# An attention and expert block on one core: P V products in groups of eight matmuls, eight P buffers, one set of exp sums, denominators at half 6

## The chip, the cores and the metric
The kernel runs on one core of one Trainium2 chip. The metric is the device time of one execution in microseconds (us). TensorE (PE) does the matmuls, VectorE (DVE) and ScalarE (ACT) read their results, GpSimd (POOL) adds, and SyncE (SP) issues most of the DMAs.

## The reference, cut to what matters
```python
# x: 4 x 1024 x 512 f32, 16 heads of 32; wq, wk, wv, wo: 512 x 512; 8 experts of rank 64
scores = einsum('bqhd,bkhd->bhqk', x @ wq.T, x @ wk.T)
att = einsum('bhqk,bkhd->bqhd', softmax(scores), x @ wv.T) @ wo.T
x = layernorm(x + att)
expert = argmax(softmax(x @ Wr.T + br)); weight = max(softmax(...))
y = ((x @ A[expert].T) @ B[expert].T) / 64 * weight
out = layernorm(x + y)
```

## The kernel before, in words
**Slots, units, halves.** The attention is done in 32 slots (4 batches of 8 head pairs). A slot has 16 units: for each of its 8 blocks of 128 keys, one unit for each head of the pair. A unit is 128 keys by 1024 queries and has two halves of 512 queries, so a slot has 32 halves and the kernel 1024. Every engine runs its own program, written out as a loop over the same halves, and semaphores tie them together.

**What a half holds on PE** (loop at lines 528 to 540): the scores matmul of this half (`score`, L493, records at L500) into one of two banks; one matmul for the row maxima of a later slot (`max_item`, L483, records at L490), 40 halves ahead, into one of three banks; in every fourth half (3, 7, 11, ...) an `out_block` (L503, records at L512): four matmuls that multiply one key block of P with V, each writing 32 of the 128 rows of the bank `pv` (two heads, two halves of the queries); and the pieces that a planner has put there (`AT`): projections Q, K, V (L400, L411), output projection (L422, L430), expert stages (L438 to L463), four chunks of one matmul each for most of them. The profile shows every f32 matmul of these as two passes, so an `out_block` has eight records and a chunk two; the matmuls for scores and maxima have one.

**The planner.** `PLAN` gives each slot three lists of pieces, one for each of `SEGMENTS` (L44), halves 0 to 10, 10 to 26 and 26 to 32; the pieces of a list are spread evenly over the halves of their segment, and `rooms` (L97) says how much each segment of a slot gets. Two pieces are pinned: `den` (L467) of the slot before at half 10, and `max_t` (L476) of the next slot at half 26. All pieces take turns on two banks `w`, and each waits until the piece two before it has been read out.

**Around the scores.** ACT reads the scores of a half and writes exp into P (`exp`, L560, records at L565), which has `NP` = 6 buffers of one unit. Before it overwrites one it waits for the P V products of that unit and for POOL's addition of it (`adds_until`, L226). POOL adds the P tiles of a slot into `Psum`, one running sum for each head (`add`, L348, 14 additions a slot, records at L354 and L358). `Psum` has two sets that slots use in turn. `den` multiplies the two sums with ones on PE (L472), ACT copies the result (`copy_den`, L585), DVE takes reciprocals in four pieces (L694) 2, 3, 5 and 6 halves later, and multiplies the copied `pv` with them (`normalise`, L698, two pieces) at `norm_half` (L223): 8 halves after `den`, or, for the first slot of a batch, at the start of the second slot behind it.

**The maxima.** DVE reduces each bank of L490 (L676). After the 32nd maximum of a slot (its matmul is issued at half 23 of the slot before) DVE combines them (L679) and writes the two parts of the negated maxima, `nm` (L684, L686). `max_t` transposes `nm` on PE at half 26 (L478), ACT copies it, and SP's DMA puts it into the stack that the scores of the next slot read.

Of the kernel before, what the change touches and what calls it, by code (L numbers as in the profile page):

```python
# [6 lines left out]
def build_attention_lora_moe_block(nc, xT, x, wqT, wkT, wvT, woT, aT, bT, wrT, br, out):  # L7
# [8 lines left out]
    D, TOK = xT.shape  # L16
    B, S, _ = x.shape
# [4 lines left out]
    KT = D // 128  # L22
    KB = S // 128
    PAIRS = H // 2
    QUADS = H // 4
# [6 lines left out]
    KS = 3 * HD + 2  # L32
    NP, NMX = 6, 3
    LEAD = 4
# [8 lines left out]
    WEIGHT = {"t1": 2, "t2": 2, "lg": 4, "den": 0, "max_t": 0}  # L43
    SEGMENTS = ((0, 10), (10, 26), (26, 32))  # L44

# [41 lines left out]
    for batch in range(B):  # L87
        at, final = PAIRS * batch, batch + 1 == B
        if batch == 0:
            PLAN[at] = (qks(0, 8, 1), qks(0, 9, 2), qks(0, 11, 1))  # L90
            PLAN[at + 1] = (qks(0, 12, 1), qks(0, 13, 2), qks(0, 15, 1))
        else:
            PLAN[at] = (tiles("v", batch, 4, 2), tiles("v", batch, 6, 2) + tiles("o", batch - 1, 0, 1), tiles("o", batch - 1, 1, 1))
            PLAN[at + 1] = (tiles("o", batch - 1, 2, 2), tiles("o", batch - 1, 4, 3), tiles("o", batch - 1, 7, 1))
        fill = qks(batch + 1, 0, 14) if not final else []
        pieces = expert_pieces(batch - 1, fill) if batch else fill
        rooms = ([2, 3, 1] if batch else [0, 4, 2]) + [2, 3, 1] * 4  # L97
        parts_of = spread(pieces, rooms)
        for n in range(5):
            PLAN[at + 2 + n] = tuple(parts_of[3 * n:3 * n + 3])  # L100
        PLAN[at + 7] = (tiles("part", 0, 0, 2), tiles("part", 0, 2, 4), tiles("part", 0, 6, 2)) if final else \
            (qks(batch + 1, 14, 2), tiles("v", batch + 1, 0, 3), tiles("v", batch + 1, 3, 1))

# [36 lines left out]
    with ctx:  # L140
# [16 lines left out]
        stack0, stack1 = sb("stack0", [128, 3, 2, S], f32r), sb("stack1", [128, 2, 2, S], f32r)  # L157
        V, P, Psum = sb("V", [128, KB, D]), sb("P", [128, NP, S]), sb("Psum", [128, 2, 2, S])
        attT = sb("attT", [128, KT, S])
# [174 lines left out]
        def _(pool):  # L334
# [13 lines left out]
            def add(s, k):  # L348
                unit, i = UNITS * s + k, k % 2
                pool.wait_ge(exp_done, 2 * unit + 2)  # L350
                if k < 4:
                    if s > 1:
                        pool.wait_ge(den_done, s - 1)
                    pool.tensor_tensor(Psum[:, s % 2, i, :], P[:, (unit - 2) % NP, :], P[:, unit % NP, :],  # L354
                                       ALU.add).then_inc(add_done, 1)
                else:
                    pool.wait_ge(add_done, ADDS * s + k - 3)
                    pool.tensor_tensor(Psum[:, s % 2, i, :], Psum[:, s % 2, i, :], P[:, unit % NP, :],  # L358
                                       ALU.add).then_inc(add_done, 1)
# [26 lines left out]
        def _(pe):  # L386
# [80 lines left out]
            def den(s, _, bank):  # L467
                pe.wait_ge(add_done, ADDS * (s + 1))
                for c in range(2):
                    for i in range(2):  # L470
                        at = HD * (2 * c + i)
                        done = pe.matmul(bank[at:at + HD, :], ones[:, :], Psum[:, s % 2, i, 512 * c:512 * c + 512],  # L472
                                         start=True, stop=True)
# [28 lines left out]

            def out_block(s, kb):  # L503
                pe.wait_ge(exp_done, 2 * (UNITS * s + 2 * kb + 2))
                if s % PAIRS == 0:
                    pe.wait_ge(v_done, KB * (s // PAIRS) + kb + 1)
                if kb == 0 and s:
                    pe.wait_ge(pv_copied, s)
                for c in range(2):
                    for i in range(2):  # L510
                        at, head = HD * (2 * c + i), 2 * (s % PAIRS) + i
                        done = pe.matmul(pv[at:at + HD, :], V[:, kb, HD * head:HD * head + HD],  # L512
                                         P[:, (UNITS * s + 2 * kb + i) % NP, 512 * c:512 * c + 512],
                                         start=(kb == 0), stop=(kb == KB - 1))
                done.then_inc(pv_done, 1)
# [12 lines left out]
            for half in range(HALVES * SLOTS):  # L528
# [5 lines left out]
                if c == 1 and k == 1 and s:  # L534
                    out_block(s - 1, KB - 1)
                if c == 1 and k % 2 == 1 and k >= 3:
                    out_block(s, (k - 3) // 2)
                for kind, n, chunk in AT.get(half, ()):
                    bank = begin((kind, n), False) if chunk == 0 else BANK[kind, n]
                    KIND[kind](n, chunk, bank)  # L540
            out_block(LAST, KB - 1)
            pe.wait_ge(exp_done, 2 * UNITS * SLOTS)
# [11 lines left out]
        def _(act):  # L554
# [5 lines left out]
            def exp(unit, c):  # L560
                if c == 0 and unit >= NP:
                    act.wait_ge(pv_done, (unit - NP) // 2 + 1)
                    act.wait_ge(add_done, adds_until(unit - NP))
# [9 lines left out]
            def copy_v(n):  # L573
                act.wait_ge(v_ready, n + 1)
                if n >= KB:
                    act.wait_ge(pv_done, KB * (PAIRS * (n // KB) - 1) + n % KB + 1)
                act.activation(V[:, n % KB, :], BANK["v", n][:, :], ACT.Copy).then_inc(v_done, 1)

            def copy_out(s):
                act.wait_ge(pv_done, KB * (s + 1))  # L580
                if s:
# [275 lines left out]
```

## Time and profile before
| | us |
|---|---|
| median of 3 runs (lowest, highest) | 1752.55 (1750.02, 1756.64) |
| the profiled execution | 1753.8 |
| its span, first to last instruction | 1751.9 |

A row of the timeline has the start in us, the duration in us, the engine, the line of the kernel, the operation with what it writes and reads, and how many records are merged into it; the bracket behind it is the idle time of that engine before it and who ended it. Rows of the kind PE are matmuls, whose ends are modelled, so distances between starts are used here rather than durations. Rows of a stretch give the busy time of each engine in it, then the granted clock of TensorE as a share of 2.4 GHz.

### The profile page before, as it was taken

The numbers are of one execution on the slowest core, as the hardware profiler recorded it, in microseconds if no ns is written. First come the engines' busy times: TensorE is split into PE (matmuls) and PEld (weight loads), VectorE is DVE, ScalarE is ACT, GpSimd is POOL, SyncE is SP. The second block draws the span as 40 slices with busy tenths as digits, with TensorE's granted clock in tenths as the row PEclk, the third lists the DMA queues.
The fourth block names the chain that finished last, engine by engine and source line by source line (L and its number), as shares of the span: only waits on it lengthen the run. The fifth ranks groups of instructions, "written<-read, shape, count | busy, mean of one in ns | idle before, by whom it ended". The sixth has DMA issues, their size and how long they took to land.

```text
span 1751.9 us, 19084 instructions
## 1 busy us (share of the span) xinstructions
PE 1610.9 (92%) x6432; PEld 765.0 (44%) x6432; DVE 1159.7 (66%) x1875; ACT 772.1 (44%) x1409; POOL 1109.0 (63%) x591
## 2 busy tenths in 40 slices
PE   5979899999999998899999999889999898889897
PEld 2434344444444444444444444444444444443353
DVE  1656777776676667866676776677666777776542
ACT  1134445454444444445445444444544544445322
POOL 1057777887676666566677765557767866768610
PEclk9989999999999999999999999999999999999999
DMA  7333432342032221135231122321313112210001
GB/s 239 97 121 91 134 95 72 86 114 60 20 84 61 73 73 57 40 92 148 51 85 41 34 84 61 85 50 65 116 37 85 38 37 49 49 31 14 0 1 48
DMA packets 64799, 123.40 MB, mean 70 GB/s; under 512 B 5296, under 2 KB 22720, under 8 KB 64704
## 3 DMA queue, kind: packets, MB, share of 16 engines
q1 hardware_dynamic: 61440, 116.94, 24.0%
q0 software_dynamic: 1152, 4.22, 0.7%
q10 hardware_dynamic: 2112, 1.05, 0.2%
q8 instruction: 51, 0.84, 0.2%
q14 instruction: 44, 0.36, 0.1%
HBM read 79.71 MB, written 41.94 MB: 69 GB/s over the span
## 4 chain that ended last, share of the span: by engine, by line
PE 72%; DVE 18%; issue 5%; POOL 2%; DMA 1%; ACT 1%; SPq 0%; ACTq 0%; POOLq 0%; DVEq 0%
PE w L400 12%; PE sc L500 12%; PE pv L512 12%; PE mx L490 11%; DVE mxc L676 6%; PE w L411 6%; PE w L422 5%; PE w L463 4%; PE w L450 4%; DVE attT L704 3%; DVE rden L696 2%; POOL Psum L358 2%; DVE split L691 1%; DMA wqk_s<-wkT 1%; PE w L444 1%
## 5 line engine op out<-in xcount | busy, mean ns | idle before, releaser
L358 POOL TENSOR_TENSOR Psum<-Psum,P 128x1024 f32<-128x1024 f32 x384 | 912.7, 2389 | 241.0 <-ACT P L565 239.6
L676 DVE TENSOR_REDUCE mxc<-mx 128x1 f32<-128x512 f32 x1024 | 676.2, 680 | 445.9 <-PE mx L490 441.0
L565 ACT ACTIVATE P<-sc 128x512 f32<-128x512 f32 x1024 | 594.8, 596 | 695.2 <-PE sc L500 688.3
L500 PE MATMUL sc<-stack 98*128 98x512 f32 x1024 | 688.6, 673 | 12.1 <-DMA stack<-mrow 10.3
L490 PE MATMUL mx<-stack 96*128 96x512 f32 x1024 | 419.8, 413 | 27.1 <-DVE mxc L676 26.9
L500 PEld LDWEIGHTS sc<-stack 98*128 98x128 f32 x1024 | 196.2, 192 | 296.8 <-issue 148.4
L354 POOL TENSOR_TENSOR Psum<-P 128x1024 f32<-128x1024 f32 x64 | 151.1, 2369 | 264.3 <-ACT P L565 264.0
L400 PE MATMUL w<-xT_s,wqk_s 128*128 128x512 f32 x512 | 271.4, 622 | 27.1 <-DMA wqk_s<-wkT 17.8
L490 PEld LDWEIGHTS mx<-stack 96*128 96x128 f32 x1024 | 198.6, 194 | 202.0 <-issue 138.0
L512 PE MATMUL pv<-P,V 128*32 128x512 f32 x2048 | 279.3, 618 | 0.0
L400 PEld LDWEIGHTS w<-xT_s,wqk_s 128*128 128x128 f32 x512 | 94.1, 195 | 112.9 <-issue 86.0
L411 PE MATMUL w<-wv_s,xT_s 128*128 128x512 f32 x256 | 130.5, 598 | 1.5 <-DVE split L691 1.2
L463 PE MATMUL w<-b_s,hmT 128*128 128x512 f32 x216 | 115.6, 624 | 10.2 <-DVE hm L765 6.1
L696 DVE RECIPROCAL rden<-rden 128x128 f32<-128x128 f32 x128 | 119.7, 938 | 3.4 <-ACT rden L589 3.4
L450 PE MATMUL w<-a_s,yT 128*128 128x512 f32 x208 | 114.5, 638 | 2.3 <-DVE split L691 1.2
L422 PE MATMUL w<-wo_s,attT 128*128 128x512 f32 x196 | 102.1, 603 | 10.7 <-DVE r L726 8.8
L704 DVE TENSOR_TENSOR attT<-pv_s,rden 64x512 f32<-64x512 f32 x64 | 97.2, 1519 | 1.5
L367 POOL TENSOR_TENSOR ve<-mv,eps_s 128x2 f32<-128x2 f32 x32 | 7.3, 227 | 126.6 <-DVE mv L715 126.6
L512 PEld LDWEIGHTS pv<-P,V 128*32 128x32 f32 x2048 | 40.7, 109 | 96.7 <-issue 89.1
L571 ACT ACTIVATE split<-w 128x512 fp32r<-128x512 f32 x64 | 38.2, 597 | 79.5 <-PE w L400 79.5
L691 DVE TENSOR_TENSOR split<-w,split 128x512 fp32r<-128x512 f32 x64 | 43.7, 683 | 39.4 <-ACT split L571 39.2
L411 PEld LDWEIGHTS w<-wv_s,xT_s 128*128 128x128 f32 x256 | 47.4, 190 | 28.4 <-issue 11.2
(107 smaller groups left out, 887.5 us busy)
## 6 DMA issues: line engine op xcount, KB each, us to landing
stack<-qk_parts SPq DMA_DIRECT2D x192, 256.0 KB, 5.5
qk_parts<-split SPq DMA_DIRECT2D x64, 512.0 KB, 2.8
xT_s<-xT SPq DMA_DIRECT2D x8, 1024.0 KB, 10.2
r<-x SPq DMA_DIRECT2D x3, 2048.0 KB, 9.3
out<-r SPq DMA_DIRECT2D x12, 512.0 KB, 3.8
wqk_s<-wqT SPq DMA_DIRECT2D x14, 256.0 KB, 4.0
wqk_s<-wkT SPq DMA_DIRECT2D x14, 256.0 KB, 4.4
xT_s<-x SPq DMA_DIRECT2D x1, 2048.0 KB, 11.8
```

The costliest lines, as they stand in the source:

```text
L358: pool.tensor_tensor(Psum[:, s % 2, i, :], Psum[:, s % 2, i, :], P[:, unit % NP, :], ALU.add).then_inc(add_done, 1)
L400: done = pe.matmul(bank[:, :], wqk_s[:, j % 2, kind, kt, :], xT_s[:, kt, 512 * c:512 * c + 512], start=(kt == 0), stop=(kt == KT - 1))
L411: done = pe.matmul(bank[:, :], xT_s[:, kt, 128 * kb:128 * kb + 128], wv_s[:, kt, :], start=(kt == 0), stop=(kt == KT - 1))
L422: done = pe.matmul(bank[:, :], attT[:, kt, 128 * t:128 * t + 128], wo_s[:, kt, :], start=(kt == 0 or only), stop=(kt == KT - 1))
L450: done = pe.matmul(bank[:, :], yT[:, 128 * kt:128 * kt + 128], a_s[:, kt, :], start=(kt == 0), stop=(kt == KT - 1))
L463: done = pe.matmul(bank[:, :], hmT[:, 128 * kt:128 * kt + 128], b_s[:, kt, :], start=(kt == 0), stop=(kt == KT - 1))
L490: pe.matmul(mx[g % NMX][:, :], stack(q, i)[0:3 * HD, 1, 128 * qb:128 * qb + 128], stack(q, i)[0:3 * HD, 0, 512 * c:512 * c + 512], start=T ...
L500: pe.matmul(sc[c][:, :], stack(s, i)[0:KS, 0, 128 * kb:128 * kb + 128], stack(s, i)[0:KS, 1, 512 * c:512 * c + 512], start=True, stop=True ...
L512: done = pe.matmul(pv[at:at + HD, :], V[:, kb, HD * head:HD * head + HD], P[:, (UNITS * s + 2 * kb + i) % NP, 512 * c:512 * c + 512], star ...
L565: act.activation(P[:, unit % NP, 512 * c:512 * c + 512], sc[c][:, :], ACT.Exp).then_inc(exp_done, 1)
L676: dve.tensor_reduce(mxc[:, q % 2, m:m + 1], mx[g % NMX][:, :], AX.X, ALU.max).then_inc(mx_done, 1)
L696: dve.reciprocal(rden[:, 128 * n:128 * n + 128], rden[:, 128 * n:128 * n + 128]).then_inc(rden_done, 1)
```

## The change
The P V products of two key blocks are issued together, `out_group` with eight matmuls at halves 11, 19, 27 and half 3 of the next slot, in place of `out_block` with four at every fourth half. P has eight buffers instead of six. `Psum` has one set, so the first additions of a slot wait for `den` of the slot before. The first segment ends at half 6 instead of 10, which moves `den` there, and with it the copy, the reciprocals and (where they follow it) the multiplications by four halves; the planner's lists are shared out anew, so that the first segment has less and the second more.

```diff
-    NP, NMX = 6, 3
+    NP, NMX = 8, 3
-    SEGMENTS = ((0, 10), (10, 26), (26, 32))
+    SEGMENTS = ((0, 6), (6, 26), (26, 32))
...
-            PLAN[at] = (tiles("v", batch, 4, 2), tiles("v", batch, 6, 2) + tiles("o", batch - 1, 0, 1), tiles("o", batch - 1, 1, 1))
-            PLAN[at + 1] = (tiles("o", batch - 1, 2, 2), tiles("o", batch - 1, 4, 3), tiles("o", batch - 1, 7, 1))
+            PLAN[at] = (tiles("v", batch, 4, 1), tiles("v", batch, 5, 3) + tiles("o", batch - 1, 0, 1), tiles("o", batch - 1, 1, 1))
+            PLAN[at + 1] = (tiles("o", batch - 1, 2, 1), tiles("o", batch - 1, 3, 4), tiles("o", batch - 1, 7, 1))
-        rooms = ([2, 3, 1] if batch else [0, 4, 2]) + [2, 3, 1] * 4
+        rooms = ([1, 4, 1] if batch else [0, 5, 1]) + [1, 4, 1] * 4
-        PLAN[at + 7] = (tiles("part", 0, 0, 2), tiles("part", 0, 2, 4), tiles("part", 0, 6, 2)) if final else \
-            (qks(batch + 1, 14, 2), tiles("v", batch + 1, 0, 3), tiles("v", batch + 1, 3, 1))
+        PLAN[at + 7] = (tiles("part", 0, 0, 1), tiles("part", 0, 1, 6), tiles("part", 0, 7, 1)) if final else \
+            (qks(batch + 1, 14, 1), qks(batch + 1, 15, 1) + tiles("v", batch + 1, 0, 3), tiles("v", batch + 1, 3, 1))
...
-        V, P, Psum = sb("V", [128, KB, D]), sb("P", [128, NP, S]), sb("Psum", [128, 2, 2, S])
+        V, P, Psum = sb("V", [128, KB, D]), sb("P", [128, NP, S]), sb("Psum", [128, 2, S])
...
                 if k < 4:
-                    if s > 1:
-                        pool.wait_ge(den_done, s - 1)
-                    pool.tensor_tensor(Psum[:, s % 2, i, :], P[:, (unit - 2) % NP, :], P[:, unit % NP, :],
+                    if s:
+                        pool.wait_ge(den_done, s)
+                    pool.tensor_tensor(Psum[:, i, :], P[:, (unit - 2) % NP, :], P[:, unit % NP, :],
...
-            def out_block(s, kb):
-                pe.wait_ge(exp_done, 2 * (UNITS * s + 2 * kb + 2))
+            def out_group(s, g):
+                pe.wait_ge(exp_done, 2 * (UNITS * s + 4 * g + 4))
                 if s % PAIRS == 0:
-                    pe.wait_ge(v_done, KB * (s // PAIRS) + kb + 1)
-                if kb == 0 and s:
+                    pe.wait_ge(v_done, KB * (s // PAIRS) + 2 * g + 2)
+                if g == 0 and s:
                     pe.wait_ge(pv_copied, s)
-                for c in range(2):
-                    for i in range(2):
-                        at, head = HD * (2 * c + i), 2 * (s % PAIRS) + i
-                        done = pe.matmul(pv[at:at + HD, :], V[:, kb, HD * head:HD * head + HD],
-                                         P[:, (UNITS * s + 2 * kb + i) % NP, 512 * c:512 * c + 512],
-                                         start=(kb == 0), stop=(kb == KB - 1))
+                for kb in (2 * g, 2 * g + 1):
+                    for c in range(2):
+                        for i in range(2):
+                            at, head = HD * (2 * c + i), 2 * (s % PAIRS) + i
+                            done = pe.matmul(pv[at:at + HD, :], V[:, kb, HD * head:HD * head + HD],
+                                             P[:, (UNITS * s + 2 * kb + i) % NP, 512 * c:512 * c + 512],
+                                             start=(kb == 0), stop=(kb == KB - 1))
                 done.then_inc(pv_done, 1)
...
                 if c == 1 and k == 1 and s:
-                    out_block(s - 1, KB - 1)
-                if c == 1 and k % 2 == 1 and k >= 3:
-                    out_block(s, (k - 3) // 2)
+                    out_group(s - 1, GROUPS - 1)
+                if c == 1 and k % 4 == 1 and k >= 5:
+                    out_group(s, (k - 5) // 4)
...
-                    act.wait_ge(pv_done, (unit - NP) // 2 + 1)
+                    act.wait_ge(pv_done, (unit - NP) // 4 + 1)
```
`GROUPS` is 4. ACT's other waits on `pv_done` (for V and for the copy of `pv`) are counted in groups in the same way.

## Rows read from the trace of the kernel before
**Rows 1.** The page: busy time of each engine and share of the span
```profile
PE 1610.9 (92%) x6432; PEld 765.0 (44%) x6432; DVE 1159.7 (66%) x1875; ACT 772.1 (44%) x1409; POOL 1109.0 (63%) x591
```
**Rows 2.** The page: the chain that ended last, by engine and by line
```profile
PE 72%; DVE 18%; issue 5%; POOL 2%; DMA 1%; ACT 1%; SPq 0%; ACTq 0%; POOLq 0%; DVEq 0%
PE w L400 12%; PE sc L500 12%; PE pv L512 12%; PE mx L490 11%; DVE mxc L676 6%; PE w L411 6%; PE w L422 5%; PE w L463 4%; PE w L450 4%; DVE attT L704 3%; DVE rden L696 2%; POOL Psum L358 2%; DVE split L691 1%; DMA wqk_s<-wkT 1%; PE w L444 1%
```
**Rows 3.** Stretches: all slots, slot 6, slot 8; clock behind the busy times
```profile
106.00:1647.00 1541.00, 1445.82 (x5938) 682.63 (x5937) 1073.67 (x1677) 730.52 (x1331) 1087.66 (x542) 0.98 0.24 67
351.70:389.70 38.00, 37.11 (x163) 17.03 (x161) 30.20 (x45) 20.31 (x39) 33.78 (x15) 1.00 0.35 97
437.10:486.00 48.90, 46.98 (x187) 21.88 (x185) 31.27 (x44) 22.18 (x40) 32.99 (x15) 1.00 0.15 33
```
**Rows 4.** Timeline, PE: maxima matmuls around a half with a chunk, and without
```profile
713.70 0.40 PE L490 MATMUL mx<-stack 96*128 96x512 f32 x1
715.04 0.40 PE L490 MATMUL mx<-stack 96*128 96x512 f32 x1
...
182.84 0.40 PE L490 MATMUL mx<-stack 96*128 96x512 f32 x1
183.32 0.40 PE L490 MATMUL mx<-stack 96*128 96x512 f32 x1
```
**Rows 5.** Timeline, PE and weight loads: a half with `out_block`; one block's two passes
```profile
470.52 0.40 PE L490 MATMUL mx<-stack 96*128 96x512 f32 x1
470.85 0.16 PEld L512 LDWEIGHTS pv<-P,V 128*32 128x32 f32 x8 [0.37 <-issue]
472.19 0.40 PE L490 MATMUL mx<-stack 96*128 96x512 f32 x1
...
705.13 0.64 PE L512 MATMUL pv<-P,V 128*32 128x512 f32 x4
...
705.58 0.61 PE L512 MATMUL pv<-P,V 128*32 128x512 f32 x4
```
**Rows 6.** The page, costliest groups: POOL's additions, ACT's exps
```profile
L358 POOL TENSOR_TENSOR Psum<-Psum,P 128x1024 f32<-128x1024 f32 x384 | 912.7, 2389 | 241.0 <-ACT P L565 239.6
L565 ACT ACTIVATE P<-sc 128x512 f32<-128x512 f32 x1024 | 594.8, 596 | 695.2 <-PE sc L500 688.3
L354 POOL TENSOR_TENSOR Psum<-P 128x1024 f32<-128x1024 f32 x64 | 151.1, 2369 | 264.3 <-ACT P L565 264.0
```
**Rows 7.** Timeline: from the last maximum to the transpose, slot 8
```profile
471.40 2.36 POOL L358 TENSOR_TENSOR Psum<-Psum,P 128x1024 f32<-128x1024 f32 x1 [0.93 <-ACT P L565]
471.98 1.81 DVE L684 TENSOR_SCALAR nm<-mm 128x16 fp32r<-128x16 f32 x1
473.82 0.18 DVE L686 SCALAR_TENSOR_TENSOR nm<-mm,nm 128x16 fp32r<-128x16 f32 x1
475.09 0.27 PE L478 MATMUL w<-ident,nm 128*32 128x128 f32 x1
```
**Rows 8.** Timeline: the same in slot 0
```profile
120.29 7.05 POOL L358 TENSOR_TENSOR Psum<-Psum,P 128x1024 f32<-128x1024 f32 x3
121.02 0.40 PE L490 MATMUL mx<-stack 96*128 96x512 f32 x1
125.07 2.30 DVE L686 SCALAR_TENSOR_TENSOR nm<-mm,nm 128x16 fp32r<-128x16 f32 x1
127.52 0.27 PE L478 MATMUL w<-ident,nm 128*32 128x128 f32 x1 [1.78 <-DVE nm L686]
```
**Rows 9.** Timeline of slot 3, DVE and PE; then a stretch behind it
```profile
248.40 1.96 DVE L704 TENSOR_TENSOR attT<-pv_s,rden 64x512 f32<-64x512 f32 x1
251.00 2.15 DVE L704 TENSOR_TENSOR attT<-pv_s,rden 64x512 f32<-64x512 f32 x1
253.80 0.49 PE L490 MATMUL mx<-stack 96*128 96x512 f32 x1 [2.04 <-DVE mxc L676]
...
254.70:258.10 3.40, 3.40 (x13) 1.50 (x5) 3.23 (x6) 0.60 (x1) 2.98 (x2) 0.50 0.00 0
```

More of the change, by code:

```diff
@@ L23, in build_attention_lora_moe_block @@
     KB = S // 128
+    GROUPS = KB // 2
     PAIRS = H // 2
@@ L357, in add @@
                     pool.wait_ge(add_done, ADDS * s + k - 3)
-                    pool.tensor_tensor(Psum[:, s % 2, i, :], Psum[:, s % 2, i, :], P[:, unit % NP, :],
+                    pool.tensor_tensor(Psum[:, i, :], Psum[:, i, :], P[:, unit % NP, :],
                                        ALU.add).then_inc(add_done, 1)
@@ L471, in den @@
                         at = HD * (2 * c + i)
-                        done = pe.matmul(bank[at:at + HD, :], ones[:, :], Psum[:, s % 2, i, 512 * c:512 * c + 512],
+                        done = pe.matmul(bank[at:at + HD, :], ones[:, :], Psum[:, i, 512 * c:512 * c + 512],
                                          start=True, stop=True)
@@ L540, in _ @@
                     KIND[kind](n, chunk, bank)
-            out_block(LAST, KB - 1)
+            out_group(LAST, GROUPS - 1)
             pe.wait_ge(exp_done, 2 * UNITS * SLOTS)
@@ L575, in copy_v @@
                 if n >= KB:
-                    act.wait_ge(pv_done, KB * (PAIRS * (n // KB) - 1) + n % KB + 1)
+                    act.wait_ge(pv_done, GROUPS * (PAIRS * (n // KB) - 1) + n % KB // 2 + 1)
                 act.activation(V[:, n % KB, :], BANK["v", n][:, :], ACT.Copy).then_inc(v_done, 1)
             def copy_out(s):
-                act.wait_ge(pv_done, KB * (s + 1))
+                act.wait_ge(pv_done, GROUPS * (s + 1))
                 if s:
```

## The prediction
> **What bounds the kernel now.** I read the page's busy shares first: PE is busy 92% of the span, POOL 63%, DVE 66% [rows 1]. The chain that ended last says whether that share matters: 72% of it is PE, 18% DVE, and the P V products alone are 12% [rows 2]. The stretches by slot show the same from near by: in slot 8 PE is busy 46.98 of 48.90 us, and in slot 6, a light one with few pieces, 37.11 of 38.00 [rows 3]. POOL is busy 33.78 of those 38.00 us, so in the light slots a second engine is close behind. Then I read distances between starts of the maxima matmul, which comes once in every half. A half with nothing else takes 0.48 us, one with a chunk 1.34 [rows 4], one with an `out_block` 1.67 (470.52 to 472.19) [rows 5]. PE's time is thus a sum of fixed prices, and what cuts a price where PE is on the chain cuts the kernel.
>
> **The groups of eight.** An `out_block` costs 1.67 - 0.48 = 1.19 us [rows 4, 5]. It has four matmuls side by side in two passes, and the second pass starts 0.45 after the first (705.13, 705.58) [rows 5]. Two passes at 0.45 are 0.90, so 0.29 of the 1.19 is paid for going into this form of matmul and out again. No row shows eight matmuls in one group. The nearest is the step from the first pass to the second: same tiles, same bank, new weights, 0.45. I take it for the two further steps, so a pair costs 1.19 + 0.90 = 2.09 instead of 2.38. There are 4 x 32 = 128 pairs: **-37 us**. The bounds are -37 - 3 (steps as cheap as half a chunk, (1.34 - 0.48)/2 = 0.43) and 0 (the second block pays the entry again). Most of it lies on the chain: 12% of 1752 is 210 us [rows 2], of 256 x 1.19 = 305 with the steps in and out; what doesn't is in the second rival below.
>
> **Less room in front of `max_t`.** This is what the change gives back. From the last maxima matmul of a slot (half 23) to the transpose at half 26 PE had 4.57 us in slot 8 (470.52 to 475.09) [rows 5, 7], because half 23 held an `out_block`. In the new order half 23 holds none; the group is at 19 and 27. PE then gets there after 0.24 (that matmul's own step, half of 0.48), the chunks of halves 23 to 25 at 0.86 each, and three times 0.48. By the planner's formula there is one chunk in slots 0 to 6: 2.5 us. In 14 later slots there are two: 3.4. In two it is 3.0, in the eight heaviest three chunks: 4.2. What DVE needs for it is 3.48 (470.52 to 474.00) plus 0.13 to start the transpose, of which 1.81 is the first `nm` instruction: it ends within 0.03 of the end of POOL's addition (471.40 + 2.36) [rows 7]. A DVE instruction of this kind is thus held until POOL's addition ends. In slot 0, where POOL ran three additions without a gap (7.05), the second `nm` instruction was held as well, 2.30, and the chain took 6.35 (121.02 to 127.37) [rows 8]. So a light slot waits 3.6 - 2.5 = 1.1, or, held twice, 6.5 - 2.5 = 4.0. I take four of the seven with one hold and three with two: 4.4 + 12 = 16. Of the others 14 wait 0.2 and two 0.6: 4. **+20 us**; bounds 0 (POOL pauses at the right moment; the least would be 3.48 - 1.63) and 7 x 4.0 + 24 x 3.1 = 102 (held twice everywhere).
>
> **One set of sums.** POOL's first addition of a slot needs the exp of half 5, and now also `den` at half 6, so it starts one half and a `den` later, about 0.48 + 1.19 less the 0.3 or so that it would have waited: 1.3 us. Queued behind it on POOL are the slot's other 13 additions. 14 x 2.39 = 33.5 [rows 6] and that start make 35 us, against a slot 6 of 38.0 - 1.2 (four pairs) = 36.8, so POOL doesn't set the pace, but with little left it runs gapless for much of a light slot; in slot 8, 33.5 of 48.9, it catches up at once. P's eight buffers let ACT be eight units ahead of POOL instead of six, so exp doesn't wait. `den` itself waits for the last addition, which ends some 3 us after the last exp, while PE has six halves (6 x 0.48, chunks, and a group, over 6 us) in front of it: **0**. If that cover went, each wait would stop scores too. ACT's copy of `den` waits for the multiplications of the slot before, which now come at half 14 of that slot: 0. What is gapless on POOL is why I let three of seven light slots be held twice.
>
> **A wait long enough for the clock.** PE waited 2.04 us at 253.80, and from 254.70 on the granted clock was 0.50 (1.2 GHz) for 3.40 us [rows 9], after 1.00 before. That costs about half of it, 1.7. Three waits of 4.0: **+5**.
>
> **Reciprocals and multiplications four halves earlier.** The same instructions (4 and 2 a slot), 1.96 and 2.15 us for the two multiplications, again held by POOL [rows 9]. In slot 3 they stood directly in front of the last maxima, and the stop of 2.04 and the slow clock followed, 3.7 together. Four halves earlier they have a whole group of PE time between them and the last maxima. I count **-6** for the light slots; bounds -15 (four such stops gone) and +10 (the stops only move, and those of the slots with experts grow). SP's DMAs aren't moved: loads and the store of maxima keep their halves.
>
> **Spreading and ends.** The planner's pieces are the same, so their prices are. Halves with nothing in them go from 204 to 275, but runs of two or more, where ACT's exps of 0.60 [rows 6] would hold PE, go from 26 to 27 by the planner's formula: 0. At the very end the last group waits for the last exp with both blocks: **+1**.
>
> Sum: -37 + 20 + 5 - 6 + 1 = -17. The profiled execution took 1753.8 for a span of 1751.9, within 1.3 us of the median, 1752.55; from the median I forecast **1735 us**.
>
> **Rivals.**
> - *The gain stays.* POOL pauses where `nm` wants to run, the stops vanish: -37 + 10 - 8 = -35, 1718 us. For it: in slots 7 onwards POOL has time to spare. Against: the 2.5 us.
> - *DVE takes over.* 18% of the chain is DVE, more where the experts' small instructions are. If half of the 37 runs into them and the transposes cost their 20: 1753 us. A gap that the faster PE reaches earlier is still a gap.
> - *Slower: `max_t` everywhere.* If POOL, started late by `den`, is gapless at half 23 in most slots, the transpose waits 4.0 seven times and 3.1 some twelve times, with the slow clock (1.7) each time: 28 + 37 + 32 = 97, less 37: 1812 at worst; with half of these slots 1764. It decides from waits of 46 us in all. Against: slot 8's POOL is idle a third of the time [rows 3].
> - *The second block pays its way in again.* Then the 37 are gone, and the waits stay: 1770 us. The row speaks against it: eight weight loads start within 0.16 us, four of them for the second pass [rows 5]. The Trainium skill, "TensorE: Matmul & The Clock Gate", part 3, says that LDWEIGHTS overlap with running matmuls only when the row group differs; all of these use all 128 rows, so by that rule every pass would wait for its loads and grouping would bring little. By the trace they do overlap (the first pass runs on to 705.77 by its row). That the third pass's loads behave otherwise can't be seen there.
>
> **Numbers.** The forecast case 0.40 (its own range 1725 to 1744), gain stays 0.20, DVE takes over 0.22, `max_t` everywhere 0.12, entry paid again 0.06. A measurement of this kernel can tell about 0.5%, 8.8 us, from no change. Faster by more: the first two, 0.60. Within it: DVE takes over, 0.22. Slower: the last two, 0.18. The range leaves out the lowest tenth and the worse half of the slower ones (those past 1764): 1715 to 1766.
>
> **What would show it.** Right: a half with a group 2.57 us from maxima matmul to maxima matmul, passes 0.45 apart through all four; PE's waits at L478 at about 1.1 or 4.0 us in slots 0 to 6, ended by L686; POOL's first addition released by `den`. Wrong: a group costing 2.38; waits of several us in slots 7 and up; or L478 without waits and the gain over 30 us. DVE's share of the chain much over 18% would be the second rival.

## The result and the profile after
The changed kernel takes 1904.34 us (median of 4 runs, 1900.82 to 1906.22) against 1751.43 us before: a ratio of 1.0865, with a 95% interval of 1.0836 to 1.0893. It is slower by 153 us, where 1735 and no more than 1766 was forecast. The profiled execution has a span of 1903.2 us, and its mean granted clock is 0.931 of 2.4 GHz, before 0.975.

First the page: the busy times, and the chain that ended last by engine and by line, which answer to [rows 1, 2].
```profile
PE 1645.8 (86%) x6432; PEld 805.7 (42%) x6432; DVE 1248.3 (66%) x1875; ACT 769.2 (40%) x1409; POOL 1107.8 (58%) x591
...
PE 64%; DVE 26%; issue 6%; ACT 1%; DMA 1%; POOL 1%; SPq 0%; ACTq 0%; DVEq 0%; POOLq 0%
PE pv L515 13%; PE w L401 11%; PE mx L491 10%; PE sc L501 9%; DVE mxc L679 9%; PE w L423 4%; PE w L412 4%; PE w L464 4%; DVE attT L707 3%; DVE nm L687 3%; PE w L451 3%; DVE rden L699 2%; DVE nm L689 2%; DVE gate L760 2%; DVE eq L755 2%
```
POOL's work is the same (1107.8 us, before 1109.0), its share smaller. The chain has moved to DVE: 18% of 1752 are 315 us, 26% of 1903 are 495.

Were the groups of eight dearer than thought? The timeline of PE around one of them in slot 7, at a granted clock of 1.00:
```profile
480.35 0.50 PE L491 MATMUL mx<-stack 96*128 96x512 f32 x1 [0.81 <-DVE mxc L679]
480.78 1.92 PE L515 MATMUL pv<-P,V 128*32 128x512 f32 x16
482.63 0.70 PE L412 MATMUL w<-wv_s,xT_s 128*128 128x512 f32 x1
```
Sixteen records in 1.85 us to the next chunk. A half that holds only a group takes 2.52 us in the trace, so the group costs 2.52 - 0.47 = 2.05 instead of the 2.09 of the forecast. The gain is there. The time was lost in waits, and at the slower clock behind them. The waits of PE, longest in total first (us, times, longest), of the kernel after and then of the kernel before:
```profile
PE mx L491 <- DVE mxc L679: 64.6, 37, 5.4
PE w L479 <- DVE nm L689: 46.8, 18, 4.8
PE w L458 <- DVE r L736: 20.2, 10, 4.8
```
```profile
PE mx L490 <- DVE mxc L676: 26.9, 20, 2.4
PE w L457 <- DVE r L733: 14.6, 13, 2.9
```
And DVE's instructions, in the groups by line (count, busy us, mean ns), again after and then before:
```profile
L707 DVE TENSOR_TENSOR attT<-pv_s,rden 64x512 f32<-64x512 f32 x64 | 124.0, 1937 | 1.5
L687 DVE TENSOR_SCALAR nm<-mm 128x16 fp32r<-128x16 f32 x32 | 55.5, 1734 | 3.3
L689 DVE SCALAR_TENSOR_TENSOR nm<-mm,nm 128x16 fp32r<-128x16 f32 x32 | 45.4, 1418 | 1.1
L760 DVE TENSOR_SCALAR gate<-eq,eqm,lrec 128x8 f32<-128x8 f32 x32 | 44.4, 1389 | 1.2
L755 DVE SCALAR_TENSOR_TENSOR eq<-lsb,lmax,rank 128x8 f32<-128x8 f32 x32 | 34.6, 1081 | 0.0
```
```profile
L704 DVE TENSOR_TENSOR attT<-pv_s,rden 64x512 f32<-64x512 f32 x64 | 97.2, 1519 | 1.5
L684 DVE TENSOR_SCALAR nm<-mm 128x16 fp32r<-128x16 f32 x32 | 45.1, 1411 | 3.3
L757 DVE TENSOR_SCALAR gate<-eq,eqm,lrec 128x8 f32<-128x8 f32 x32 | 27.7, 867 | 1.2
L752 DVE SCALAR_TENSOR_TENSOR eq<-lsb,lmax,rank 128x8 f32<-128x8 f32 x32 | 26.8, 839 | 0.0
L686 DVE SCALAR_TENSOR_TENSOR nm<-mm,nm 128x16 fp32r<-128x16 f32 x32 | 11.9, 373 | 1.1
```
The same 192 instructions took 209 us before and 304 after. The timeline of slot 5 shows what that does (POOL, DVE and PE's maxima matmul), and the last row, of the stretches, what follows (PE, PEld, DVE, ACT, POOL busy, then the granted clock):
```profile
364.76 11.63 POOL L359 TENSOR_TENSOR Psum<-Psum,P 128x1024 f32<-128x1024 f32 x5
...
369.34 7.59 DVE L707 TENSOR_TENSOR attT<-pv_s,rden 64x512 f32<-64x512 f32 x1
...
376.86 0.68 DVE L679 TENSOR_REDUCE mxc<-mx 128x1 f32<-128x512 f32 x1
...
377.59 0.80 PE L491 MATMUL mx<-stack 96*128 96x512 f32 x1 [5.24 <-DVE mxc L679]
...
378.00:381.40 3.40, 2.71 (x11) 0.78 (x14) 3.21 (x6) 0.60 (x1) 1.87 (x1) 0.50 0.39 154
```
POOL adds without a pause from 364.76 to 376.39. A multiplication of DVE that takes 0.68 us by itself begins at 369.34 and ends only when POOL has run dry. It was held over four additions. The maxima pile up behind it, the three banks fill, PE stands for 5.24 us, and the clock is at 1.2 GHz when it goes on.

**A balance by halves.** Here and below, "fixed prices" are what a half costs when nothing waits, from distances between scores matmuls (0.47 bare, 0.85 more for each chunk, 1.19 for a block, 2.05 for a group, and so on), summed over the planner's 1023 distances; "stops" are the rest of the measured distances. Before: 1397 + 153 us. After: 1357 + 344. So the fixed prices fell by 40, near the 37 of the forecast, and the stops rose by 191. The stops of one place depend somewhat on the prices chosen; differences between two kernels hardly do. By place, over all slots:

| halves of the slot | stops before | stops after |
|---|---|---|
| 12 to 17 | 14 | 48 |
| 18, 19 | 1 | 82 |
| 21 to 24 | 51 | 9 |
| 25 | 4 | 12 |
| 26, 27 (transpose and behind it) | 52 | 153 |

The slow clock is within these: (1 - 0.931) x 2 x 1903 = 263 us at 1.2 GHz, before (1 - 0.975) x 2 x 1752 = 88. Work done there takes twice its time, so the 175 us more cost at most 87 of the 153 lost. Within the slots (from 110 us on) the trace has 41 stretches at 1.2 GHz, 242 us in all, with PE busy for 203 of them; before it has 13, 65 us, with PE busy for 57. By PE's busy time the difference is (203 - 57)/2 = 73 us.

### The profile page after: what moved, and what is told of

It reads as the page before. It is cut to its first block, busy times and chain, and to the rows that moved or that the text cites. A ratio compares the mean times of both kernels' runs of the same rounds, so it can differ in the third digit from the quotient of the medians.

```text
span 1903.2 us, 19068 instructions
## 1 busy us (share of the span) xinstructions
PE 1645.8 (86%) x6432; PEld 805.7 (42%) x6432; DVE 1248.3 (66%) x1875; ACT 769.2 (40%) x1409; POOL 1107.8 (58%) x591
## 4 chain that ended last, share of the span: by engine, by line
PE 64%; DVE 26%; issue 6%; ACT 1%; DMA 1%; POOL 1%; SPq 0%; ACTq 0%; DVEq 0%; POOLq 0%
PE pv L515 13%; PE w L401 11%; PE mx L491 10%; PE sc L501 9%; DVE mxc L679 9%; PE w L423 4%; PE w L412 4%; PE w L464 4%; DVE attT L707 3%; DVE nm L687 3%; PE w L451 3%; DVE rden L699 2%; DVE nm L689 2%; DVE gate L760 2%; DVE eq L755 2%
## 5 line engine op out<-in xcount | busy, mean ns | idle before, releaser
L359 POOL TENSOR_TENSOR Psum<-Psum,P 128x1024 f32<-128x1024 f32 x384 | 911.9, 2393 | 370.3 <-ACT P L568 369.4
L679 DVE TENSOR_REDUCE mxc<-mx 128x1 f32<-128x512 f32 x1024 | 669.3, 679 | 504.2 <-PE mx L491 501.6
L491 PE MATMUL mx<-stack 96*128 96x512 f32 x1024 | 429.5, 422 | 64.8 <-DVE mxc L679 64.6
L401 PE MATMUL w<-xT_s,wqk_s 128*128 128x512 f32 x512 | 277.6, 635 | 41.3 <-DMA wqk_s<-wkT 18.0
L501 PEld LDWEIGHTS sc<-stack 98*128 98x128 f32 x1024 | 200.4, 196 | 259.5 <-issue 186.8
L515 PE MATMUL pv<-P,V 128*32 128x512 f32 x2048 | 289.2, 689 | 0.0
L401 PEld LDWEIGHTS w<-xT_s,wqk_s 128*128 128x128 f32 x512 | 98.9, 202 | 109.3 <-issue 67.1
L707 DVE TENSOR_TENSOR attT<-pv_s,rden 64x512 f32<-64x512 f32 x64 | 124.0, 1937 | 1.5
L515 PEld LDWEIGHTS pv<-P,V 128*32 128x32 f32 x2048 | 58.7, 120 | 149.6 <-issue 147.1
L412 PEld LDWEIGHTS w<-wv_s,xT_s 128*128 128x128 f32 x256 | 46.9, 190 | 29.8 <-issue 18.8
```

The source lines that it names most:

```text
L359: pool.tensor_tensor(Psum[:, i, :], Psum[:, i, :], P[:, unit % NP, :], ALU.add).then_inc(add_done, 1)
L401: done = pe.matmul(bank[:, :], wqk_s[:, j % 2, kind, kt, :], xT_s[:, kt, 512 * c:512 * c + 512], start=(kt == 0), stop=(kt == KT - 1))
L412: done = pe.matmul(bank[:, :], xT_s[:, kt, 128 * kb:128 * kb + 128], wv_s[:, kt, :], start=(kt == 0), stop=(kt == KT - 1))
L491: pe.matmul(mx[g % NMX][:, :], stack(q, i)[0:3 * HD, 1, 128 * qb:128 * qb + 128], stack(q, i)[0:3 * HD, 0, 512 * c:512 * c + 512], start=T ...
L501: pe.matmul(sc[c][:, :], stack(s, i)[0:KS, 0, 128 * kb:128 * kb + 128], stack(s, i)[0:KS, 1, 512 * c:512 * c + 512], start=True, stop=True ...
L679: dve.tensor_reduce(mxc[:, q % 2, m:m + 1], mx[g % NMX][:, :], AX.X, ALU.max).then_inc(mx_done, 1)
```

## The experiments
The two theories at this point: DVE instructions held by POOL stop PE (theory 1), or the groups of eight, or the late start of POOL behind one set of sums, do it in some other way. Ratios are to the kernel before on the same chip, with 95% intervals.

### Is it the hold at all?
POOL's additions cut to 16 columns, in the changed kernel and in the kernel before. The sums over the keys are left out for all other columns, which are set to 1 once:
```diff
-                    pool.tensor_tensor(Psum[:, i, :], Psum[:, i, :], P[:, unit % NP, :],
+                    pool.tensor_tensor(Psum[:, i, 0:16], Psum[:, i, 0:16], P[:, unit % NP, 0:16],
```


> The changed kernel with POOL's additions cut to 16 of 1024 columns (the sums over keys are left out for the rest), so that POOL holds no DVE instruction for long. All waits and the order stay. Theory 1 (DVE instructions held by POOL's additions, then PE's stops, then the slow clock): the stops at halves 18, 19, 26 and 27 go; the fixed prices of the halves add up to 1362 us, with some 60 us of stops and 200 outside the slots the run takes about 1625 us. Rival (the groups or the banks themselves stop PE): it stays above 1800.

> The kernel before with the same cut of POOL's additions (the sums over keys are left out but for 16 columns). Theory 1: the fixed prices add up to 1397 us, so about 1660 us, 35 us more than the changed kernel with the same cut; this difference is what the groups of eight are worth when nothing is held. Rival: the two differ the other way round, by 100 us or more.


Measured: 1657.3 us (0.9441, 0.9401 to 0.9482) and 1677.1 us (0.9554, 0.9521 to 0.9587). The order turns round: with nothing held, the changed kernel is 20 us faster. Both times are above what was expected (1625 and 1660), and the difference is 20 instead of 35, since the changed kernel keeps 18 us more of stops even so. The multiplications of the changed kernel with the cut:
```profile
L708 DVE TENSOR_TENSOR attT<-pv_s,rden 64x512 f32<-64x512 f32 x64 | 43.7, 683 | 1.5
```
Stops are 95 and 77 us; the other 250 of the changed kernel came with POOL's long additions. The rival that groups stop PE by themselves falls.

### Which part of the change?
Groups, eight buffers and one set, but the segments and lists of before; then the new segments and lists and one set with blocks of four and six buffers; then, later, groups and nothing else:
```diff
# e3_group_only_den10, against the changed kernel (lists likewise)
-    SEGMENTS = ((0, 6), (6, 26), (26, 32))
+    SEGMENTS = ((0, 10), (10, 26), (26, 32))
# g1_groups_pure: this, and
-    NP, NMX = 8, 3
+    NP, NMX = 6, 3
-                    if s:
-                        pool.wait_ge(den_done, s)
-                    pool.tensor_tensor(Psum[:, i, :], P[:, (unit - 2) % NP, :], P[:, unit % NP, :],
+                    if s > 1:
+                        pool.wait_ge(den_done, s - 1)
+                    pool.tensor_tensor(Psum[:, s % 2, i, :], P[:, (unit - 2) % NP, :], P[:, unit % NP, :],
```


> The changed kernel with the segments and the planner's lists of before (den at half 10), groups of eight, eight buffers and one set of sums kept. If the groups alone do it (no P V products at half 23, so PE reaches the transpose early, and additions bunched behind a group): above 1850 us, with the waits at the transpose as in the changed kernel. If the new place of den and of the pieces does it: near 1730 us. In this kernel POOL starts a slot at half 10, which should make it worse still.

> The kernel before (blocks of four, six buffers) with the new segments and lists (den at half 6) and one set of sums. If the groups do it: within 1% of before, 1745 to 1765 us, with the 153 us of stops of before. If the late start of POOL and the multiplications at halves 14 and 15 do it: above 1850 us.

> Groups of eight and nothing else: six buffers, two sets of sums, den at half 10 and the lists of before. If one set of sums (POOL's late start) is what makes POOL gapless: 1720 to 1760 us, far below the 1935 of the kernel that differs by the one set. If the groups bunch the exps and leave half 23 bare whatever the sums do: above 1820.


Measured: 1935.47 (1.1026, 1.0936 to 1.1117), 1811.73 (1.0321, 1.0286 to 1.0357) and 1829.83 us (1.0451, 1.0421 to 1.0480). Both halves of the change lose by themselves: the new segments with one set 56 us, the groups alone 79, and 56 + 79 = 135 is most of the 153. The first and the third came out above the bounds set for groups as a cause (1850 and 1820); the second fell between its two values (1765 and 1850), so I had wrongly expected one part to do all of it. One set with eight buffers costs 106 us on top of groups when `den` stays at half 10 (1935 against 1830): POOL then starts its additions at half 10. DVE's instructions tell the two parts apart:

| | second `nm`, us in all | multiplications, longest | of over 3 us |
|---|---|---|---|
| before | 11.9 | 2.82 | 0 |
| new segments, one set, blocks of four | 12.0 | 6.43 | 5 |
| groups alone | 45.4 | 2.93 | 0 |
| both (the changed kernel) | 45.4 | 7.61 | 5 |

The groups have the second `nm` held; the late start behind one set has multiplications held over several additions.

The groups alone lose at the transpose. PE waits there for `nm` 40.5 us in 20 waits. nm's second instruction, which was 0.373 on average before:
```profile
L689 DVE SCALAR_TENSOR_TENSOR nm<-mm,nm 128x16 fp32r<-128x16 f32 x32 | 45.4, 1420 | 1.1
```
Half 26 and 27 have 143 us of stops there, before 52. In the changed kernel the timeline of slot 8 reads (answering to [rows 7]):
```profile
536.65 7.06 POOL L359 TENSOR_TENSOR Psum<-Psum,P 128x1024 f32<-128x1024 f32 x3 [2.17 <-ACT P L568]
...
539.63 1.82 DVE L687 TENSOR_SCALAR nm<-mm 128x16 fp32r<-128x16 f32 x1
...
541.48 2.27 DVE L689 SCALAR_TENSOR_TENSOR nm<-mm,nm 128x16 fp32r<-128x16 f32 x1
...
543.89 0.27 PE L479 MATMUL w<-ident,nm 128*32 128x128 f32 x1 [2.21 <-DVE nm L689]
```
POOL idled 2.17 us, since PE spent 2.05 in the group at half 19 and gave no scores, and then it had three additions in a row just where nm wants to run. In the kernel before, an addition every 3 us left a gap in the same place of slot 8. This is a heavy slot, which the forecast had down for one hold.

### The parts of the wait: place of the transpose, of the multiplications, of the groups
```diff
# e5_after_maxt28
-    SEGMENTS = ((0, 6), (6, 26), (26, 32))
+    SEGMENTS = ((0, 6), (6, 28), (28, 32))
# e10_after_norm12
-            return HALVES * (s + 2) if s % PAIRS == 0 else den_half(s) + 8
+            return HALVES * (s + 2) if s % PAIRS == 0 else den_half(s) + 12
# e11_groups_early
-                if c == 1 and k == 1 and s:
+                if c == 1 and k == 0 and s:
...
-                if c == 1 and k % 4 == 1 and k >= 5:
-                    out_group(s, (k - 5) // 4)
+                if c == 1 and k % 4 == 0 and k >= 4:
+                    out_group(s, (k - 4) // 4)
```


> The changed kernel with max_t pinned at half 28 (and its store at 29), two halves and a group of eight later. Theory 1: the 120 + 33 us of stops at halves 26 and 27 go, the group at 27 gives the time; those at 18 and 19 stay: 1740 to 1790 us, unless the scores of the next slot now wait for the maxima (4 us from the copy to the first score in the lightest slot of before). Rival (the stops only move to the next DVE instruction that is held): above 1850 us.


Measured: 1883.71 us (1.0743, 1.0721 to 1.0765). Theory 1 missed: 21 us, not 115 to 165. The rival's value (above 1850) came. The stops at halves 18 and 19 stayed, and those at 26 and 27 moved on to 27 and 28. PE no longer waits for the transpose, but for the maxima, 114.6 us instead of 64.6:
```profile
PE mx L491 <- DVE mxc L679: 114.6, 54, 6.8
```

> The changed kernel with the multiplications 12 halves after den instead of 8, at halves 18 and 19 as before. If their place in front of the group at 19 makes the 82 us of stops at halves 18 and 19: these go or shrink, and stops at 22 to 26 grow as in the kernel before, 1850 to 1890 us. If the place doesn't matter (POOL is gapless at both): the same 1904 within 15.


Measured: 1818.36 us (1.0371, 1.0348 to 1.0393). The multiplications at halves 14 and 15 cost 86 us more than at 18 and 19. Stops at 18 and 19 are gone, those at 22 and 23 are back (43 us). More went than the 1850 of the expectation: the second `nm` took 28.6 us instead of 45.4, and the wait at L479 fell to 29.8. Why they did is not shown. The hold of the multiplications did not get shorter: in slots 3 to 6 the first of each pair took 8.2 to 8.4 us, where it took 7.5 to 7.6 at halves 14 and 15. What differs is the work that PE has behind them: at the later place the group of half 19 follows at once. That this is the reason is argued, not shown.

> The changed kernel with each group of eight one unit earlier, at halves 9, 17, 25 and 1, so that a group lies between the last maxima matmul (23) and the transpose (26). Theory 1 (too little room for the held nm instructions): the 153 us of stops at halves 26 and 27 fall below 60, and the time comes to 1790 to 1830. Rival (POOL is gapless there in any case, the group's own bunch of exps included, and nm is held until it runs dry): the stops move with it, within 20 us of 1904.


Measured: 1765.47 us (1.0090, 1.0068 to 1.0112), 139 us less than the changed kernel for moving each group by two halves, and below the expected 1790. The wait for the transpose:
```profile
PE w L479 <- DVE nm L689: 9.6, 8, 2.5
```
before this edit 46.8 us in 18 waits. DVE's nm instructions are nearly as long as they were (47.9 and 45.7 us, before 55.5 and 45.4), so the hold is hardly shorter. PE has the 2.05 us of a group to do in the meantime. This is the room that half 23 lost. It is not all of the 139: some 86 us of stops went at halves 26 and 27, and some 55 at 18 and 19, where the group at half 17 now stands behind the multiplications.

```diff
# e14_norm12_lead5, e13_early_norm12_lead5 (the first without, the second with the early groups)
-    LEAD = 4
+    LEAD = 5
```


> The same with the multiplications 12 halves after den (18 and 19). If the two causes are separate, the gains add up: 1904 - 86 (as the later multiplications alone gave) - 90 = about 1730 us, which would be below the kernel before. If they are one (how much POOL is gapless): no lower than 1790.

> The changed kernel with the multiplications 12 halves after den, and the maxima 42 halves ahead instead of 40, so that the last one is issued at half 21. Theory 1: two more halves of room at the transpose, about 2 us in 31 slots, of the 115 us of stops at halves 26 and 27 that the later multiplications left; 1818 - 60 = about 1760 us. Rival (held until POOL runs dry): the multiplications at 18 and 19 stand right in front of the nm instructions at 21 now, 1800 us or more.

> All three: groups one unit earlier, multiplications 12 halves after den, maxima 42 halves ahead. Theory 1: 1700 to 1725 us, below the kernel before, with the fixed prices at 1357 and under 150 us of stops. If the room was enough already: the same as without the longer lead.


Measured: 1776.14 (1.0152, 1.0113 to 1.0190), 1810.00 (1.0339, 1.0287 to 1.0392) and 1816.50 us (1.0380, 1.0347 to 1.0414). The values of theory 1 (1730, 1760, 1700 to 1725) missed all three times; the second came out at its rival's (1800 or more), the other two at neither. The gains don't add up, and with the early groups the later multiplications lose 11 us. A longer lead puts the last maximum at half 21, right behind multiplications at 18 and 19, and nm then comes late behind them. In these runs moving one step on DVE moved the stop.

### What ends a hold?
Each addition as four of 256 columns:
```diff
+                    for q in range(4):
+                        c = slice(256 * q, 256 * q + 256)
+                        done = pool.tensor_tensor(Psum[:, i, c], Psum[:, i, c], P[:, unit % NP, c], ALU.add)
+                    done.then_inc(add_done, 1)
```


> The changed kernel with each of POOL's additions issued as four of 256 columns, nothing left out. Theory 1 (a DVE instruction is held until the running addition ends): a hold is at most 0.65 us instead of 2.4, so the 304 us that DVE spends in multiplications, nm, gate and eq fall towards 110, most stops of over 2 us and their slow clock go, and the time comes to 1690 to 1730 us. Rival (POOL takes the port from DVE for as long as it has work, in one piece or four): no shorter holds, above 1850 us.

> The kernel before with the same four pieces. Theory 1: 1700 to 1735 us, 10 to 30 above the changed kernel with the same pieces, as with the small additions (1677 against 1657). If it is below that kernel, the groups of eight lose even with short holds.


Measured: 1878.61 (1.0718, 1.0695 to 1.0741) and 1805.47 us (1.0312, 1.0284 to 1.0339). Theory 1 in its first form, that a hold always ends with the running instruction, falls here, and with it the times that it forecast (1690 to 1735). Nor is the changed kernel the faster one, as it was with the small additions; since long holds stayed in both, that says nothing of the groups with short ones. From the timeline of the changed kernel with four pieces:
```profile
483.42 11.67 POOL L363 TENSOR_TENSOR Psum<-Psum,P 128x256 f32<-128x256 f32 x17
...
489.12 6.01 DVE L691 TENSOR_SCALAR nm<-mm 128x16 fp32r<-128x16 f32 x1
```
Seventeen short additions, a possible end every 0.7 us, and DVE waits 6.01 us until POOL has none left (483.42 + 11.67 = 495.09, DVE ends at 495.13). Such a hold ended where POOL paused. But it is the rarer kind.

In the changed kernel 116 of the 192 instructions were held (0.9 us or more, with the end of an addition inside). 107 of them ended with the addition that was running, 51 of these with the next one right behind it (as at 541.45 in slot 8 above, within a run of three). Nine went on over two to four additions: the first `nm` in slots 0 and 1 (4.95 and 5.65 us), a multiplication in slots 3 to 6 and 29, an `eq` and a `gate`. With four pieces most holds did shrink, the median multiplication from 1.96 to 1.07 us, the first `nm` from 1.82 to 0.44, and no second `nm` took over 0.66. But 23 of the 192 took over 3 us, up to 13.1, and these keep the total at 284 us instead of 304. In the kernel before, where no hold was longer than 2.82 us, four pieces made 14 of over 3 us. What decides whether a hold goes on is not settled.

Four pieces also cost POOL more, 1073.8/384 = 2.80 us for each later addition instead of 911.9/384 = 2.37, so that it pauses less; the two effects are not separated here.

The Trainium skill, "SBUF — State Buffer", section "Who interferes with whom", says that a VectorE instruction with two SBUF inputs, or in a two-port mode, shares a port with GpSimd, that the one that issues first keeps it for its whole instruction, and that tensor_reduce never contends. The trace agrees on which instructions are held (the combining reduction took 0.19 in every slot, nm up to 5.65). On how long it agrees for the 107 holds that ended with one addition, and differs for the others: 6.01 and 7.59 us are several instructions, not one.

### Taking the hold away
The reductions suggest the remedy: nm, which was a tensor_scalar and a scalar_tensor_tensor, as four reductions over one or two elements.
```diff
-                    dve.tensor_scalar(nm[:, :, 0, :], mm[:, :, :], -1.0, None, ALU.mult).then_inc(comb_done, 1)
...
+                    dve.tensor_reduce(nm[:, :, 0, :], mm[:, :, :].unsqueeze(3), AX.X, ALU.max, negate=True).then_inc(comb_done, 1)
+                    dve.tensor_reduce(neg[:, :, :, 0], mm[:, :, :].unsqueeze(3), AX.X, ALU.max, negate=True).then_inc(comb_done, 1)
...
+                    dve.tensor_reduce(neg[:, :, :, 1], nm[:, :, 0, :].bitcast(f32).unsqueeze(3), AX.X, ALU.max,
+                                      negate=True).then_inc(comb_done, 1)
...
+                    dve.tensor_reduce(nm[:, :, 1, :].bitcast(f32), neg[:, :, :, :], AX.X, ALU.add).then_inc(comb_done, 1)
```


> The changed kernel with the two nm instructions written as four small reductions over mm (nothing left out). The combining reduction in front of them took 0.19 us in every slot, held never, so these should take 0.2 each and the transpose finds them ready. If the hold of nm is what stops PE at halves 26 and 27: those 153 us go but for some 35 that the small additions left there too, and the time is 1904 - 118 = about 1785 us. If DVE is late there for another reason (behind the multiplications): above 1870.

> The kernel before with the same four reductions. Of its 49 us of stops at half 26 the small additions left 35, so little is there to gain: 1730 to 1750 us by the theory of the hold, the same 1751 if its nm was never late enough to matter.


Measured: 1788.25 (1.0213, 1.0184 to 1.0242) and 1735.48 us (0.9913, 0.9893 to 0.9934). Each reduction takes 0.16 to 0.19 us:
```profile
L694 DVE TENSOR_REDUCE nm<-neg 128x16 f32<-128x32 f32 x32 | 6.0, 186 | 1.1
L688 DVE TENSOR_REDUCE nm<-mm 128x16 fp32r<-128x16 f32 x32 | 5.4, 170 | 3.4
```
The hold of nm is worth 116 us in the changed kernel and 15 in the kernel before. Stops at 26 and 27 are 48 us instead of 153. This shows the larger part of the loss, 116 of 153 us, with one edit that leaves the order on PE, the groups and the sums as they are.

> Groups of eight with six buffers, two sets and the lists of before, one unit earlier (halves 9, 17, 25, 1), and nm by reductions. If the room, the late start and the hold of nm are the causes, all are gone: 1705 to 1730 us, below the kernel before. If the groups bunch POOL's additions around the multiplications at 18 and 19 all the same: 1750 or more.


Measured: 1780.64 us (1.0175, 1.0151 to 1.0198). The 1705 to 1730 missed; the rival's value (1750 or more) came. With `den` at half 10 and the multiplications at 18 and 19, early groups at 17 and 25 leave some 90 us of stops at halves 21 to 23, and three multiplications took over 3 us, up to 7.04, though there are two sets: the late start behind one set is not the only way to such a hold.

### Both remedies on the changed kernel
```diff
# h1_mult_at_start: early groups, nm by reductions, and
-            return HALVES * (s + 2) if s % PAIRS == 0 else den_half(s) + 8
+            return HALVES * (s + 2) + 2 if s % PAIRS < PAIRS - 1 and s + 2 < SLOTS else den_half(s) + 8
```


> The changed kernel with groups one unit earlier and nm by reductions: only the multiplications at 14 and 15 and the experts' gate are still held. From the 1765 of the earlier groups, less the rest of the hold of nm: 1710 to 1740 us. If the earlier groups had already given nm its room: 1765.

> The same, and the multiplications moved to halves 2 and 3 of the slot behind, where POOL has ended its last addition of a slot (3 to 3.6 us into the slot) and waits for den (until 8 to 12 us): slots 7 of each batch, and the last two, keep 8 halves after den. If the hold until POOL runs dry is the whole cause, the multiplications take 0.68 each, the stops at 16 to 19 go, and it runs in 1665 to 1705 us, below the kernel before by 3% or more. If PE stops as much without held instructions: as the other, 1710 or more.


Measured: 1707.36 (0.9737, 0.9695 to 0.9779) and **1689.51 us (0.9663, 0.9623 to 0.9703)**. The first is just below its range, the second within it. Both beat the kernel before, the second by 62 us. Where POOL pauses is seen from its waits in that kernel, and what the multiplications then take from its groups by line:
```profile
POOL Psum L356 <- PE w L474: 212.9, 31, 9.3
```
```profile
L711 DVE TENSOR_TENSOR attT<-pv_s,rden 64x512 f32<-64x512 f32 x64 | 56.7, 886 | 1.5
```
```profile
PE mx L492 <- DVE mxc L680: 7.7, 7, 2.1
```
The one set of sums makes POOL wait 213 us for `den`, 31 times, and this wait, which seemed a mere cost, is where DVE's multiplications run freely: 53 of the 64 take 0.67 to 0.69, and PE's wait for the maxima is 7.7 us instead of 64.6. Its clock is 0.982. Fixed prices of 1357 and 129 us of stops: against the kernel before, -40 and -24. The move has a cost too: PE's scores now wait for ACT's exps 17.8 us in 22 waits, against 3.1 without it. No run has these two edits to DVE with blocks of four, so what the groups are worth beside them is known from the fixed prices alone.

## Why the prediction was wrong
**The groups of eight: right.** -37 was forecast, 40 measured in fixed prices (2.05 for a group, the steps within it 0.45 and less). The lower bound was added up wrongly: two steps at 0.43 instead of 0.45 are 5 us over 128 pairs, not 3, which gives -42. The rival that the second block pays its way in again falls: sixteen records in 1.85 us. The Trainium skill, "TensorE: Matmul & The Clock Gate", part 3, says that weight loads overlap with running matmuls only where the row group differs. For this form of matmul the trace differs: in a group of slot 5 that runs from 364.11 for 1.92 us, the loads of the later passes start at 364.56 and 364.99, with the passes 0.45 apart or less. In time the gain is seen only with the small additions, 20 us.

**Less room in front of `max_t`: the mechanism right, the size wrong.** This step failed first. It priced the hold as what one addition leaves (1.81, or 2.30 more for a second). It took one hold for the 24 heavier slots, from slot 8 of the kernel before, whose POOL paused there. But the groups change when POOL pauses: it starves during a group and works off the bunch behind it. That interplay is in no term of the sum. Measured, PE's wait at L479 was 25.7 us in slots 0 to 6, where 16 was forecast: 3.4 in each of slots 2 to 6, held twice every time, and 4.1 and 4.8 in slots 0 and 1, where the first `nm` was held for 4.95 and 5.65. In the other slots it was 21.1 us in 11 waits, where 4 was forecast: nm was held twice there too, as in slots 7 and 8. And the wait at the transpose is not the whole price: with +20 and +5 for the clock in the sum, halves 26 and 27 cost 101 us more, and taking the hold from nm alone gave 116.

**The multiplications: wrong sign.** -6 with bounds of -15 and +10 was forecast. Putting them back gave 86 us. The forecast saw that a group's time would lie between them and the last maxima. It did not see that POOL, started late by `den`, runs without a pause there in the light slots, so that one multiplication is held over several additions. The forecast said that POOL is gapless for much of a light slot, in the step on one set of sums, and used it for `nm` only. The bound rested on [rows 9], 2.15 us for a hold, and the longest was 7.61. Nor did it see what the old place had: a hold of 8.2 to 8.4 us at halves 18 and 19 stops PE less than one of 7.5 at 14 and 15, where only chunks and bare halves follow until the group at 19.

**One set of sums: 0 forecast for the exps and `den`, nearly right; what it does to DVE, wrong.** PE has no wait for `den`'s sum. ACT's exps waited 29.7 us for POOL instead of 5.6, of which 4.4 reached PE's scores. The new segments with one set and blocks of four lose 56 us.

**The clock: right in kind, too small in size.** Three falls were forecast, 5 us; 175 us more were spent at 1.2 GHz, which cost 73 to 87. The number of falls was wrong (28 more in the slots), and so was the price: 1.7 came from one stretch of 3.4 us, and the 41 stretches lasted 5.9 us on average, up to 10.2.

**The rivals.** "`max_t` everywhere" was the nearest, with 0.12: it named the place, the double hold and the clock, and set 46 us of waits as the point from which it decides. The waits at L479 were 46.8 us, just at that point, yet the kernel lost 153. Its reach of 1812 at worst was short twice: 97 us was its price for the transposes in all such slots, where nm's hold alone is worth 116, and it left out the multiplications. The argument against it, that POOL is idle a third of the time in slot 8, is where reasoning by a mean share failed: what counts here is whether it is idle in the 2 us in which a DVE instruction wants to run. The sign of "DVE takes over" came as well, DVE's share of the chain at 26% instead of 18, but not its time (1753).

## What to carry to other kernels
Before making one engine's work coarser, ask what the others do in its shadow: a longer piece on PE starves POOL and then gives it a bunch, and whatever POOL holds back finds no pause. List the instructions that another engine can hold, read their shortest and longest duration in the trace, and place them where that engine waits for something, or write them in a form that isn't held. Most holds here ended with one instruction of the other engine, but the bound should be the length of its run without a pause.

## What was not expected of the hardware
A DVE instruction with two SBUF inputs (or a tensor_scalar from SBUF) was held in nine cases over two to four additions of POOL of 2.4 us each, for 7.61 us at most, and with short additions of 0.7 for up to 13.1, until POOL paused. Cutting POOL's instructions into quarters made most holds shorter and a few much longer: on average the first nm instruction rose from 1.73 to 2.24 us and the multiplications from 1.94 to 2.33, while the second nm fell from 1.42 to 0.45. Reductions over the same tiles were never held. Open: why most holds end with the running addition and some go on.
